# Second layer's tables: the blocks of Wo1 turned by VectorE instead of TensorE

## The reference, cut to what matters

```
# layer 0: 32 query heads over 8 key/value heads, width 32
q, k, v = x @ Wq0 + bq0, ctx @ Wk0 + bk0, ctx @ Wv0 + bv0
out = softmax(q k^T / sqrt(32) + mask) v
x  = layernorm(out @ Wo0 + bo0 + x) * gamma0 + beta0
# layer 1: 16 heads, width 64
a = layernorm(ctx) * gamma1 + beta1
q, k, v = x @ Wq1.T, a @ Wk1.T, a @ Wv1.T
x  = x + tanh(gate) * (softmax(q k^T / 8, over the valid keys) v) @ Wo1.T
```

## Time and profile before

| | us |
|---|---|
| median of three executions | 1791.67 |
| lowest, highest | 1790.58, 1792.87 |
| the profiled execution, its own time | 1794.66 |
| its span, first to last instruction | 1792.8 |
| TensorE busy in the span | 1725.7 |
| VectorE busy in the span | 1149.0 |

### The profile page before, as it was taken

How to read it: one execution, slowest core, us unless ns; L and a number is a source line. 1 busy time by engine, 2 the same in 40 slices (tenths; PEclk the granted TensorE clock), 3 DMA queues, 4 the chain that set the end, 5 groups by cost and what they waited for, 6 DMA issues and landing times.

```text
span 1792.8 us, 22372 instructions
## 1 busy us (share of the span) xinstructions
PE 1725.7 (96%) x8449; PEld 1432.0 (80%) x8449; DVE 1149.0 (64%) x1089; ACT 582.1 (32%) x667; POOL 1106.7 (62%) x607
## 2 busy tenths in 40 slices
PE   6899999999999799999999999999999999999998
PEld 5788887888888688888888877788888888888886
DVE  6888888888888566565656555446644664466442
ACT  4444444444445434333433323113311331133110
POOL 2677777777777857565656677436644664466331
PEclk9999999999999999999999999999999999999999
DMA  7433332323225557776777845453744464465432
GB/s 213 115 85 77 102 79 72 83 72 86 72 69 146 159 175 250 222 251 212 254 225 235 284 150 176 144 172 129 224 153 164 144 209 141 165 186 168 140 112 88
DMA packets 277487, 278.01 MB, mean 155 GB/s; under 512 B 62202, under 2 KB 230276, under 8 KB 277380
## 3 DMA queue, kind: packets, MB, share of 16 engines
q1 hardware_dynamic: 275188, 274.49, 49.9%
q10 hardware_dynamic: 2192, 2.10, 0.4%
HBM read 174.77 MB, written 101.71 MB: 154 GB/s over the span
## 4 chain that ended last, share of the span: by engine, by line
PE 58%; DVE 18%; issue 11%; POOL 7%; ACT 6%; DMA 1%; SPq 0%; POOLq 0%; DVEq 0%; ACTq 0%
PE ps L53 18%; PE ps L54 18%; PE ps L55 18%; DVE small L1059 3%; DVE pr L1079 3%; ACT pr L822 3%; DVE pT0r L1092 2%; DVE pT1r L1092 2%; DVE xT0r L990 2%; DVE xT1r L990 2%; ACT ot L816 2%; PE ps L682 1%; PE ps L690 1%; POOL xb L1339 1%; POOL y L1353 1%
## 5 line engine op out<-in xcount | busy, mean ns | idle before, releaser
L1388 POOL TENSOR_TENSOR x2Tl<-x2r,x2Th 128x1024 fp32r<-128x1024 f32 x32 | 76.8, 2400 | 291.9 <-ACT x2Th L931 291.9
L1188 DVE STREAM_TRANSPOSE x2r<-xd 128x1024 f32<-128x1024 f32 x32 | 68.8, 2150 | 211.8 <-PE ps L55 211.8
L1324 POOL TENSOR_TENSOR pr<-pr,small 128x1024 f32<-128x1024 f32 x64 | 122.8, 1919 | 105.0 <-DVE small L1085 105.0
L931 ACT CAST x2Th<-x2r 128x1024 fp32r<-128x1024 f32 x32 | 33.6, 1051 | 376.9 <-DVE x2r L1188 376.9
L1319 POOL TENSOR_TENSOR pr<-pr,small 128x1024 f32<-128x1024 f32 x64 | 123.9, 1936 | 25.5 <-DVE small L1063 25.5
L1059 DVE TENSOR_REDUCE small<-pr 128x16 f32<-128x1024 f32 x64 | 78.0, 1219 | 78.6 <-ACT pr L822 78.6
L1339 POOL TENSOR_TENSOR xb<-xb,bo 128x1024 f32<-128x1024 f32 x32 | 77.8, 2431 | 76.3 <-DMA xb<-in_x_dram 76.3
L1353 POOL TENSOR_TENSOR y<-y,bet 128x1024 f32<-128x1024 f32 x32 | 77.7, 2427 | 52.4 <-DVE y L1104 52.4
L53 PE MATMUL ps<-wo0h,oc1l 128*128 128x512 f32 x256 | 102.6, 401 | 3.6 <-DVE y L1143 3.6
L1104 DVE TENSOR_TENSOR y<-y,gam 128x1024 f32<-128x1024 f32 x32 | 54.6, 1706 | 80.0 <-ACT y L856 80.0
L53 PE MATMUL ps<-wo0h,oc0l 128*128 128x512 f32 x256 | 102.5, 401 | 2.0 <-DVE wo0l L1014 1.6
(11 more groups left out here) (370 smaller groups left out, 5473.1 us busy)
## 6 DMA issues: line engine op xcount, KB each, us to landing
o_scratch<-ot SPq DMA_DIRECT2D x256, 64.0 KB, 1.8
ocr<-o_scratch SPq DMA_DIRECT2D x16, 1024.0 KB, 7.9
xb<-in_x_dram SPq DMA_DIRECT2D x32, 512.0 KB, 6.8
x_scratch<-y SPq DMA_DIRECT2D x32, 512.0 KB, 5.3
a_scratch<-ost SPq DMA_DIRECT2D x64, 256.0 KB, 3.4
b_scratch<-ost SPq DMA_DIRECT2D x64, 256.0 KB, 5.8
xd<-x_scratch SPq DMA_DIRECT2D x128, 128.0 KB, 2.9
raw<-b_scratch SPq DMA_DIRECT2D x64, 256.0 KB, 5.6
```

What stands on the lines that cost most here:

```text
L1324: nc.gpsimd.tensor_tensor(heads(v), heads(v), mx.unsqueeze(2).to_broadcast([P, TPB * GRP, KEYS]), ALU.subtract)\
L1388: nc.gpsimd.tensor_tensor(x2T[1][:], x2r[:], f32(x2T[0][:]), ALU.subtract).then_inc(x2_lo, 1)
```

## The change

Wo1's blocks are laid out by four transfers with runs of 32 values (128 bytes), in place of one transfer with runs of 128 values (512 bytes): partition 32a + j then holds, for each of 32 values of t, the 32 values of row 32t + j of Wo1 in columns 128f + 32a onward. VectorE's 32x32 transposition of that is the turned block, which is written to `woTr`, at the place of `woTl`. VectorE does it at the end of slot s = 1, and ScalarE and VectorE split it in slot s = 2, right behind the split of the turned Wv1. TensorE's eight transpositions of each group go. The wait of TensorE's pair 1 for `woTl` stays.

```diff
@@ placements
-        wq1r, wo1r = at("wq1r", 196, [P, D]), at("wo1r", 168, [P, KT, P])
+        wq1r, wo1r = at("wq1r", 196, [P, D]), at("wo1r", 168, [P, D // 32, 32])
+        woTr = at("woTr", 176, [P, D])
@@ SP, load_w1(f)
-                sp.dma_start(wo1r[:], w["Wo1"].rearrange("(o p) c -> p o c", p=P)[:, :, P * f:P * (f + 1)])\
-                    .then_inc(w1_ld[1], 16)
+                after(sp, wo1_turned, f)
+                for a in range(4):
+                    sp.dma_start(wo1r[32 * a:32 * (a + 1)], w["Wo1"][:, P * f + 32 * a:P * f + 32 * (a + 1)]
+                                 .rearrange("(t j) i -> j t i", j=32)).then_inc(w1_ld[1], 16)
@@ TensorE, s == 2
                     project(pe, f, 1)
-                    pe.wait_ge(w1_ld[1], 16 * (f + 1))
                     after(pe, evac_a, 8 * f)
                     after(pe, evac_d, 8 * f)
-                    for k in range(KT):
-                        last = nc.tensor.transpose(TT[:, P * k:P * (k + 1)], wo1r[:, k, :], ident[:])
-                    last.then_inc(wo1_turned, 1)
@@ ScalarE, the slot after step s
+                        if s == 1:
+                            act.wait_ge(wo1_turned, f + 1)
+                            after(act, outer, 16 * f)
+                            nc.scalar.copy(woT[0][:], woTr[:]).then_inc(wo1_hi, 1)
                     elif s == 2:
-                        act.wait_ge(wo1_turned, f + 1)
-                        after(act, outer, 16 * f)
-                        nc.scalar.copy(woT[0][:], TT).then_inc(wo1_hi, 1)
                         diagonal(f, 1)
@@ VectorE, the slot after step s
+                        if s == 1:
+                            dve.wait_ge(wo1_hi, f + 1)
+                            nc.vector.tensor_tensor(woT[1][:], woTr[:], f32(woT[0][:]), ALU.subtract).then_inc(wo1_lo, 1)
                     elif s == 2:
-                        dve.wait_ge(wo1_hi, f + 1)
-                        nc.vector.tensor_tensor(woT[1][:], TT, f32(woT[0][:]), ALU.subtract).then_inc(wo1_lo, 1)
                         diagonal(f, 1)
@@ VectorE, end of slot h, behind the statistics
                 f, s = table(h)
+                if f is not None and s == 1:
+                    dve.wait_ge(w1_ld[1], 64 * (f + 1))
+                    after(dve, outer, 16 * f)
+                    nc.vector.transpose(woTr[:], wo1r[:].rearrange("p t i -> p (t i)")).then_inc(wo1_turned, 1)
```

## The result

The changed kernel takes 1804.40 us, median of six executions (1796.77 to 1808.19); the kernel before takes 1791.12 us beside it (1788.97 to 1792.87). The ratio is 1.0066, 95% interval 1.0049 to 1.0082: slower by more than the 0.2% that can be told. The forecast was 1795.4, in the range 1784.5 to 1806.

The account below looks back on a forecast made before the run. TensorE was taken to bound group 0 and the odd groups, the landing of xb and the chunk equally the three even ones; +8.1 - 3.5 - 0.9 = +3.7 us gave 1795.4, range 1784.5 to 1806.

Parts of the forecast that it names:

- rival 2: Wo1's short runs cost far more, lying 4 KB apart in DRAM or by doubling: D = 5 or more, +10 us, 1802; chance 0.18.
- VectorE's share: One more transposition per group, 1.24 us, lying in group 1 in wTl's wait for GpSimd's wqsl: costs TensorE nothing.
- D: On the load queue, the time by which everything behind the loads of Wq1 and Wo1 comes later; taken as 3 us.
- the high end: D reckoned by SP's issues of the four Wo1 transfers: 3.8 us, say 4.
- Four such make 4.8 us: SP's four Wo1 issues, priced from one 1.20 us issue of 1024 runs: 4.8 us against 0.90 before.
- 0.7 us would fall on the store behind: On SP, behind the four Wo1 issues: 0.7 us more, added in reckoning the high end.
- The low end: D reckoned by the DMA engines' busy time per packet for Wo1: 1.7 us, or 1.4 with overlap.
- The 0.87 us saved is swallowed by this wait: Even groups: TensorE's wait takes up the saving from its removed transpositions; loss taken as 2.7 us each, +8.1 for three.
- less the 1.12 of `woTl` it is 8.7: Group 2, from wqsl's end to bd1l's: 9.8 us before, 8.7 without woTl, so TensorE goes on 1.9 us later.
- Rival 1: The DMA queue has room and xb catches up: D under 0.7 us, all groups gain, 7.7 us, 1784.0; chance 0.23.
- Rival 4: VectorE itself late, transposition 2.16 us: wTl 1 us late in odd groups, +4 us, 1791.3; chance with rival 3 together 0.14.

Follow-up runs that it names:

- e4: The kernel before with its one Wo1 transfer cut into four of 32 partitions, 256 runs of 512 bytes each: 1793.38 us, ratio 1.0008.
- e8: The kernel before with only the first two of the four short-run (128-byte) Wo1 transfers, half of the blocks not loaded: 1796.02 us, ratio 1.0023.
- e10: The kernel before with Wo1 loaded by four transfers of 512 runs of 64 values (256 bytes): 1800.73 us, ratio 1.0050.
- e9: The kernel before with its one Wo1 transfer cut by partitions into twelve, bytes and 512-byte runs unchanged: 1802.56 us, ratio 1.0055.
- e2: The kernel before with Wo1 loaded by the change's four transfers of 128-byte runs, all else unchanged: 1805.17 us, ratio 1.0082.
- e7: The changed kernel with woTl made in slot s = 3 behind bd1l, TensorE waiting for it only at pair 4: 1807.15 us, ratio 1.0084.
- e5: The changed kernel with the four Wo1 transfers for groups 1 to 7 issued by ScalarE at the end of slot s = 4: 1795.69 us, ratio 1.0029.
- e3: The changed kernel with the old single Wo1 transfer of 1024 runs of 512 bytes, VectorE turning the blocks as they lie: 1788.06 us, ratio 0.9978.
- e1: The changed kernel with SP issuing the next group's four Wo1 transfers at s = 2, no longer at s = 4: 1785.65 us, ratio 0.9960.
- e11: The changed kernel unaltered, run again for the second profile: 1804.51 us, ratio 1.0070.
- e6: Like e1, with woTl made in slot s = 3, waited for only at pair 4, and group 0's Wo1 issued one slot later: 1784.32 us, ratio 0.9964.

## Why the prediction was right and where it was short

Group 2 in most of the kernels: SP's time in Wo1's issues; the time from Wq1's issue to `xb`'s, on SP; `xb`'s start on GpSimd, counted from the group's first matmul; the group's length. The last column is the difference of the medians.

| | Wo1's issues, us | Wq1 to `xb`, us | `xb` start, us | group 2, us | against before, us |
|---|---|---|---|---|---|
| before | 0.90 | 7.2 | 3.1 | 47.2 | |
| e4, four coarse | 3.22 | 7.2 | 3.2 | 47.3 | +1.0 |
| e8, two short | 1.70 | 8.4 | 4.1 | 48.3 | +4.1 |
| e10, runs of 64 | 3.52 | 9.6 | 6.2 | 51.8 | +8.3 |
| e9, twelve coarse | 6.41 | 10.0 | 6.3 | 51.9 | +10.1 |
| e2, four short | 6.06 | 9.8 | 6.3 | 52.0 | +12.8 |
| after | 6.47 | 10.6 | 8.9 | 52.6 | +13.3 |
| e7, changed, late `woTl` | 6.07 | 10.4 | 8.9 | 51.9 | +15.2 |
| e5, issued by ScalarE | (2.69 on ScalarE) | 6.6 | 3.7 | 49.3 | +3.7 |
| e3, engines alone | 0.58 | 6.5 | 3.2 | 47.2 | -4.3 |
| e1, load at s = 2 | (elsewhere) | | 2.0 | 45.9 | -6.8 |

**The number: in the range, at its edge.** Forecast were 3.7 us more than before, measured 13.3. The forecast's own range was 1790 to 1801; 1804.40 lies in the stated one because that was stretched to 1806 for rival 2. So the way it moved came from the reasoning, and that the size fell inside is owed to the widening.

**Right: what bounds what.** TensorE bounds the odd groups and group 0, and `xb` on SP's queue the even ones. The saving of 0.87 us of each group appears in the odd ones (46.2 to 45.3, 46.2 to 45.4, 46.3 to 45.5) and in group 0 (46.3 to 45.4) of the first profile; in the second group 0 took 47.0, 1.7 us of it lost to the clock. GpSimd waited 10.9, 9.5 and 10.5 us for `xb` in groups 2, 4 and 6, as the forecast's 9 to 11.

**Right: VectorE's share.** The transposition took 1.20 us (forecast 1.24), and in odd groups it lies in the wait for the lock, though now it is GpSimd's `xb` (690.58 to 692.98) that is waited for and not `wqsl`. In group 1 `wTl` began 1.05 us earlier than in the earlier trace rows, by which time TensorE was about as much ahead, took 3.31 us and ended at 694.06, before TensorE's 694.67; `wqsl`, now behind it, took 4.16 us:

```profile
688.90 1.20 DVE L1157 STREAM_TRANSPOSE woTr<-wo1r 128x1024 f32<-128x1024 f32 x1
...
690.75 3.31 DVE L1118 TENSOR_TENSOR wTl<-wTr,wTh 128x1024 fp32r<-128x1024 f32 x1 [0.35 <-ACT wTh L870]
```

**Right in kind, low in size: D.** `xb` started 3.93 us later than before, not 3.0; this is the value that was called the high end, and it came by the way of SP that led there. Of its terms, "Four such make 4.8 us", reckoned from one issue of 1.20, was mis-sized: four took 6.47, almost all of the excess in one issue of 4.26. That 0.7 us would fall on the store behind was not seen: the stores took 2.01 us in place of 2.83. The low end, 1.4 us by the engines' busy time, was no price of this at all: the engines were starved (share 0.38) while SP stood, and e9 loses nearly as much with no byte changed.

**Wrong: "The 0.87 us saved is swallowed by this wait", with no more to pay.** TensorE came 1.95 us earlier to group 2 (731.68 against 733.63), after two groups of 0.9, but the loads on SP did not (720.82 for Wq1, 720.40 before). So against TensorE `xb` was late by 3.9 + 1.95 = 5.9 us, twice D = 3. The step reckoned each group with TensorE at its old place, and took the odd groups' slack as free. It isn't: in group 1 `xb` began 2.64 us later than before, VectorE stood 4.70 us ahead of the product with gamma, and so its copy of pairs to `ost`, for which SP's stores ahead of Wq1 wait, came at 717.00, against 716.60 before. In e3, with `xb` on time, Wq1's issue moved with TensorE (719.23 and 732.47, 1.2 us earlier both). What an odd group gains is given back in the next even one, whenever something that does not move with TensorE ends last there.

**Wrong: the size of TensorE's waits.** Forecast for each even group: a wait of 1.2 us before `wTl`, TensorE at pair 1 later than before by 1.9 us, or 3.0 if `woTl` gets in ahead, and 2 to 4 us of waits in all. In group 2 the waits were 3.96 and 0.49 us, in group 4 1.5 and 3.1, in group 6 1.1 and 3.1, so 4.2 to 4.6 in all, and pair 1 of group 2 began 3.4 us later (756.41). The step "less the 1.12 of `woTl` it is 8.7" came out as 9.6: `woTl` left the chain on VectorE and held up GpSimd by 1.0 us instead. The forecast had named this and weighed it with a part of its 1.1 us.

```profile
742.50 1.53 DVE L1118 TENSOR_TENSOR wTl<-wTr,wTh 128x1024 fp32r<-128x1024 f32 x1 [0.52 <-ACT wTh L870]
...
744.14 0.55 PE L53 MATMUL ps<-normTh,wTl 128*128 128x256 f32 x1 [3.96 <-issue]
```

(The first row is of VectorE, the second of TensorE, both of the changed kernel in group 2.)

**Missing: the clock.** No step spoke of it. With the busy time of stretches of 2 us, from 640 to 1072 us, multiplied by what the clock lacked of 1.00, the account closes:

| us | TensorE idle | lost to the clock | both | against before | less 7.0 saved | next stage starts later by |
|---|---|---|---|---|---|---|
| before | 7.3 | 2.6 | 9.9 | | | |
| after | 17.8 | 5.8 | 23.6 | +13.7 | +6.7 | +6.6 |
| second profile | 18.7 | 11.1 | 29.8 | +19.9 | +12.9 | +12.9 |

So of the +12.9 us the idle time is 11.4, the clock 8.5, and the saving -7.0. The waits for `bd1l` of the kernel before, 1.2 us at the longest, were followed by no loss of clock. Of the six waits of 3.1 to 4.0 us in groups 2, 4 and 6 of the two profiles five were, and so was one of 1.6 us in the second. This can also be what spreads the six executions over 11.4 us: that is a reading of two profiles, not shown for the other executions. The kernel before spread over 3.9 us beside it, but over 8.2 in the eleven executions beside e11, and the changed kernel over 9.0 there. The Trainium skill, TensorE: Matmul & The Clock Gate, Part 1, says that an idle array goes to 1.2 GHz and that the monitor runs free of the kernel, so that the same kernel can come out differently from run to run; group 6 above agrees.

**Of the rivals** number 2 gave the nearest time (1802 for D = 5), with "an even group loses D - 0.3": by the 5.9 us against TensorE that is 5.6 for group 2, where 5.4 was measured. In groups 4 and 6 `xb` came 3.7 and 2.5 us later against TensorE than before, and they lost 4.9 and 2.3; in the second profile the three lost 6.5, 3.5 and 4.7. Its reasons, short runs 4 KB apart and doubling in the engines, are not what most of the loss needs: e9 has no short run, and a packet of 128 bytes took 13 to 15 ns. Rival 1's price, 1784.0, is what the change is worth once its transfers are out of the way: e1 1785.65, e6 1784.32. Rival 4 didn't come up, and SP's new wait for `wo1_turned` didn't hold it: in group 2 the first of the four follows Wq1's issue at once, and among SP's waits from 620 to 1010 us there is none for it.

**Open.** The 2.7 us by which e2 lies above e9 are assigned in part: in the two profiles all groups agree within 0.1 us but group 6, 52.7 against 49.3, and over the stage (640 to 1072 us) TensorE's idle time is the same, 14.8 and 14.9 us, while the clock cost 6.8 us in e2 and 4.7 in e9. In that group e2's Wo1 kept SP for 5.94 us and e9's 4.98. A small price of short runs of their own isn't excluded. Why the third issue of four is the long one isn't settled; in group 0, in front of which the queue had stood idle, the third was the long one too, but with 1.88 us. e7 is profiled in one execution of 1800.49 us, where its median is 1807.15.

## What to carry to other kernels

Price a reshaped load by the time for which the issuing engine stands in its issues, and then look at what that engine has to send next: twelve transfers of the same bytes cost 10.1 us, four with short runs 12.8, and the same four, with what the engines save, left the kernel 6.8 us faster than before where nothing waited behind them. When the stage's bound engine gets faster, the transfers don't come earlier with it unless what releases them does; count the lateness against the engine's new place. Waits of 3.1 to 5.0 us in an even group were followed by 0 to 3.1 us lost to the clock, so a forecast of a new wait needs a second term for it.

## What was not expected of the hardware

- Four transfers of 1024 runs of 128 bytes kept SyncE for 4.2 to 7.5 us behind group 0 (e2, after), with 2.5 to 4.3 us of it in the third issue; two kept it 1.70 us in group 2 and lengthened the next issues by 2 us (e8). ScalarE stood 2.7 to 10.4 us in the same four (e5).
- A packet of 128 bytes took the DMA engines 13 to 15 ns against 27 to 28 for 512 bytes: the bytes of a load cost the engines about twice as much (by these times an estimated 1.7 us more for each Wo1), and the issuer 5.6 us more in group 2.
- The same 3.1 us of idle TensorE left the granted clock at 1.00 in one execution and took it to 0.50 in another.
